# Feed-forward phase: where the second layer's weight pieces are prepared, and how the last layer norm is computed

## The reference, cut to what matters

```
x = _layernorm(x + attn(x));  x = _layernorm(x + xattn(x, ctx));  x = _layernorm(x + ffn(x))

def ffn(x):
    h = (cos(ph) + sin(ph)) * amp          # amp = sigmoid(x @ amp_w + amp_b), ph = pi * tanh(x @ ph_w + ph_b)
    for l in range(2):
        ent = (h @ ent_w[l] + ent_b[l]) @ ent_pw[l] + ent_pb[l]
        h = layer_norm(h + ent, ln3_g[l], ln3_b[l])
        t = sum over two paths of (h @ path_w[l, p] + path_b[l, p]) * (cos(phase[l, p]) + sin(phase[l, p]))
        h = layer_norm(h + t, ln4_g[l], ln4_b[l])
    return h
```

## Time and profile before

| | |
|---|---|
| median of three timed runs | 987.88 us (986.71 to 988.43) |
| profiled execution: its time, its span | 984.96 us, 983.1 us |
| granted TensorE clock over the span | 0.971 of full speed |
| busy: TensorE | 892.4 us, 91% |
| busy: VectorE | 677.2 us, 69% |
| busy: ScalarE | 550.1 us, 56% |
| busy: GpSimd | 496.7 us, 51% |
| first instruction of the feed-forward phase | 652.55 us |

### The profile page before, as it was taken

How to read it: one execution, slowest core, us unless ns; L and a number is a source line. 1 busy time by engine, 2 the same in 40 slices (tenths; PEclk the granted TensorE clock), 3 DMA queues, 4 the chain that set the end, 5 groups by cost and what they waited for, 6 DMA issues and landing times. The chain is left out here.

```text
span 983.1 us, 19518 instructions
## 1 busy us (share of the span) xinstructions
PE 892.4 (91%) x5892; PEld 735.8 (75%) x5892; DVE 677.2 (69%) x2055; ACT 550.1 (56%) x1674; POOL 496.7 (51%) x793
## 2 busy tenths in 40 slices
PE   4999999998898899999999998669899999999893
PEld 4888888887776678778777877457678778778672
DVE  4687778786785777777876766426757657667557
ACT  4756556664664566565755556427564464564461
POOL 0445555455755345454645432610665565566466
PEclk9999999999899999999999999879999999999997
DMA  4644243444665556574654636344002001001001
GB/s 155 222 144 158 98 160 128 160 160 143 210 205 145 168 159 194 166 225 121 188 170 138 181 110 197 132 167 155 0 1 85 3 1 55 32 1 40 4 0 43
DMA packets 79075, 118.53 MB, mean 121 GB/s; under 512 B 7920, under 2 KB 41744, under 8 KB 78224
## 3 DMA queue, kind: packets, MB, share of 16 engines
q1 hardware_dynamic: 78992, 117.52, 37.2%
HBM read 58.76 MB, written 17.83 MB: 78 GB/s over the span
## 5 line engine op out<-in xcount | busy, mean ns | idle before, releaser
L920 ACT ACTIVATE prob<-bank,nmax 128x128 f32<-128x128 f32 (+1 forms) x512 | 209.9, 431 | 38.5 <-DVE nmax L1049 36.9
L161 PE MATMUL bank<-w_ffn,hT 128*128 128x512 f32 x768 | 192.8, 402 | 0.0
L1049 DVE CUSTOM_DVE_ANT_0 bank<-bank,mask 128x128 f32<-128x128 f32 (+1 forms) x512 | 167.6, 383 | 4.0 <-PE bank L1225 3.7
L161 PEld LDWEIGHTS bank<-w_ffn,hT 128*128 128x128 f32 x768 | 141.5, 189 | 30.9
L161 PE MATMUL bank<-xT,w_att 128*128 128x256 f32 x864 | 124.1, 298 | 22.0 <-DVE w_att L961 10.3
L161 PEld LDWEIGHTS bank<-xT,w_att 128*128 128x128 f32 x864 | 115.4, 201 | 31.7 <-DVE xT L1037 9.7
L777 POOL TENSOR_TENSOR zone<-raw,zone 128x256 fp32r<-128x256 f32 x128 | 95.2, 776 | 65.8 <-ACT zone L900 65.8
L1237 PE MATMUL bank<-ident,prob 128*128 128x128 f32 x768 | 119.7, 279 | 4.5 <-ACT probT L933 4.4
L933 ACT ACTIVATE probT<-bank 128x512 f32<-128x512 f32 x97 | 58.3, 603 | 92.7 <-PE bank L1261 91.6
L920 ACT ACTIVATION_READ_ACCUMULATOR prob<-bank,nmax 128x1 f32 x512 | 110.0, 215 | 0.0
L1547 ACT ACTIVATE ht<-bank,cols 128x128 f32<-128x128 f32 x192 | 72.3, 457 | 66.0 <-PE bank L1715 66.0
(11 more groups left out here) (118 smaller groups left out, 1518.7 us busy)
## 6 DMA issues: line engine op xcount, KB each, us to landing
q<-stage SPq DMA_DIRECT2D x192, 128.0 KB, 2.2
k<-kstage SPq DMA_DIRECT2D x48, 256.0 KB, 3.5
x<-xres SPq DMA_DIRECT2D x16, 512.0 KB, 4.0
raw<-in_ent_wT SPq DMA_DIRECT2D x32, 256.0 KB, 3.8
raw<-in_ent_pw SPq DMA_DIRECT2D x32, 256.0 KB, 4.1
raw<-in_xT SPq DMA_DIRECT2D x8, 512.0 KB, 3.6
raw<-in_path_w SPq DMA_DIRECT2D x8, 512.0 KB, 3.7
xres<-in_x SPq DMA_DIRECT2D x8, 512.0 KB, 4.9
```

The costliest lines, as they stand in the source:

```text
L161: ins = t.matmul(out, lhs(a, k), rhs(b, k), start=first and n == 0 and m == 0, stop=last and n == len(kts) - 1 and m == 2, skip_group_chec ...
L920: ins = s.activation(prob[:, u, c * width:(c + 1) * width], banks[u][:, c * width:(c + 1) * width], ACT.Exp, scale=-1.0, bias=nmax[:, i % ...
L1049: ins = v.tensor_tensor_reduce(scored, scored, mask[:, S - width:S], scale=-1.0, scalar=3e38, op0=ALU.add, op1=ALU.min, accum_out=nmax[:, ...
```

## The change

Three things are changed.

- Stages 2 and 3 now also go through the two halves of w_raw. SP loads each of them when VectorE is done with the half's first use, behind the loads of the norm's scale and shift. GpSimd's additions for stage 3 stand behind block 0's second residual.
- Their eight pieces (numbers 8 to 15) are no longer prepared before block 0. ScalarE rounds piece 8+n right behind `hT_of(n)`, and VectorE makes its remainder right behind `unit(n+1)`, for n from 0 to 7, in block 0 alone.
- For the last stage (units 12 to 15) VectorE no longer normalises. Behind the unit's statistics it computes (y - mean)*g in one scalar_tensor_tensor (`centre`), and later y*rstd + (x + b) in a second one (`finish`), then the statistics of the last norm. GpSimd's `last_gain` goes. `finish(i)` moves into `unit(13+i)`, right behind the drain, `NORMS` alternates accordingly, and at a block's end the next block's first two `h0` stand behind the last normalise but one.

```
-    stage_raw = [w_raw[:, 0, :, :], w_raw[:, 1, :, :], y[:, :, :], ht[:, :, :, :].rearrange("p h k j -> p h (k j)")]
+    stage_raw = [w_raw[:, n % 2, :, :] for n in range(2 * NL)]
...
-    NORMS = list(range(UN - 1)) + [UN, UN - 1] + [UN + i for i in range(1, BT)]
+    NORMS = list(range(UN - BT + 1)) + [u for i in range(BT - 1) for u in (UN + i, UN - BT + i + 1)] + [UN + BT - 1]
...
             def load_stage(n):
+                if n >= 2:
+                    wait_alone(q, s_wlo, KT * (n - 1), s_passed)
                 q.dma_start(stage_raw[n], A["fd"][n // 2, n % 2][:, 0:KT, :]).then_inc(s_wraw[n], 16)
...
+            q.dma_start(lng[:, :], A["ln_g"].partition_broadcast(P)).then_inc(s_ln, 16)
+            q.dma_start(lnb[:, :], A["ln_b"].partition_broadcast(P)).then_inc(s_ln, 16)
             load_stage(2)
             load_stage(3)
-            q.dma_start(lng[:, :], A["ln_g"].partition_broadcast(P)).then_inc(s_ln, 16)
-            q.dma_start(lnb[:, :], A["ln_b"].partition_broadcast(P)).then_inc(s_ln, 16)
...
@@ gpsimd, body
-                for u in range(UN - 2):
-                    if 2 <= u:
-                        lo(u - 2)
+                for n, u in enumerate(NORMS):
+                    if 2 <= n < UN - 2:
+                        lo(n - 2)
                     rstd_of(u)
-                    if u < BT:
-                        residual(u)
-
-                last_gain(0)
-                rstd_of(UN - 2)
-                last_gain(1)
...
+                    if n < BT:
+                        residual(n)
+                    if b == 0 and n == 1:
+                        residual_of_path(1)
@@ scalar
+            def piece_hi(k):
+                n, c = divmod(k, KT)
+                if c == 0:
+                    s.wait_ge(s_wraw[n], 16)
+                    if n % 2:
+                        s.wait_ge(s_id, KT * (n // 2 + 1))
+                s.activation(W[:, 0, k * D:(k + 1) * D], stage_raw[n][:, c, :], ACT.Copy).then_inc(s_whi, 1)
...
             gates(k, 0)
-            stage_hi(2)
-            stage_hi(3)
-            s.wait_ge(s_wlo, 2 * NL * KT)
...
                     if kind == "tr":
                         hT_of(n)
+                        if b == 0 and n < 2 * KT:
+                            piece_hi(2 * KT + n)
@@ vector
+            def piece_lo(k):
+                n, c = divmod(k, KT)
+                at = slice(k * D, (k + 1) * D)
+                v.wait_ge(s_whi, k + 1)
+                v.tensor_tensor(W[:, 1, at], stage_raw[n][:, c, :], W[:, 0, at].bitcast(F32), ALU.subtract).then_inc(s_wlo, 1)
...
-            stage_lo(2)
-            stage_lo(3)
             v.wait_ge(s_pbias, 16 * NL)
-            v.wait_ge(s_wlo, 2 * NL * KT)
...
                     k.drain(("mm", u), v.tensor_tensor(y[:, i, :], banks[plan.bank(("mm", u))][:, :], bias[:, s_, :], ALU.add))
-                    if u >= 1:
+                    if u > UN - BT:
+                        finish(u - 1 - (UN - BT))
+                    elif u >= 1:
                         normalise(u - 1, s_norm)
+                    if u > UN - BT + 1:
+                        normalise(UN + u - 2 - (UN - BT), s_fin)
                     k.wait_drained(("mm", u))
                     statistics(u)
+                    if u >= UN - BT:
+                        centre(u)
+
+                def centre(u):
+
+                    i = u % BT
+                    v.wait_ge(s_agg, b * LN + number[u])
+                    v.scalar_tensor_tensor(y[:, i, :], y[:, i, :], mv[:, i, 0:1], lng[:, :], ALU.subtract, ALU.mult).then_inc(s_cen, 1)
 
                 def finish(i):
 
                     n = b * BT + (i + 1)
-                    v.wait_ge(s_g, n)
+                    v.wait_ge(s_rstd, b * LN + number[UN - BT + i])
                     v.wait_ge(s_res, n)
-                    v.tensor_tensor(y[:, i, :], y[:, i, :], xb[b % 2][:, i, :], ALU.add).then_inc(s_sum, 1)
+                    v.wait_ge(s_cen, n)
+                    v.scalar_tensor_tensor(y[:, i, :], y[:, i, :], rstd[:, i, 1:2], xb[b % 2][:, i, :], ALU.mult, ALU.add).then_inc(s_sum, 1)
...
                     if kind == "mm":
-                        if n == UN - 1:
-                            finish(0)
                         unit(n)
+                        if b == 0 and 1 <= n <= 2 * KT:
+                            piece_lo(2 * KT + n - 1)
...
-                finish(1)
-                normalise(UN, s_fin)
-                normalise(UN - 1, s_norm)
-                finish(2)
-                normalise(UN + 1, s_fin)
+                finish(BT - 1)
+                normalise(UN + BT - 2, s_fin)
                 if not last:
                     h0(k, b + 1, 0)
-                finish(3)
-                normalise(UN + 2, s_fin)
-                if not last:
                     h0(k, b + 1, 1)
-                normalise(UN + 3, s_fin)
+                normalise(UN + BT - 1, s_fin)
```

More of the change, by code:

```diff
@@ L1356, in ffn_phase @@
     s_res = sem("s3_res")
-    s_g, s_sum = sem("s3_g"), sem("s3_sum")
+    s_cen, s_sum = sem("s3_cen"), sem("s3_sum")
     s_fin = sem("s3_fin")
@@ L1434, in _, with residual_of_path @@
             g.wait_ge(s_c, 4)
-            for l in range(NL):
+            def residual_of_path(l):
                 g.wait_ge(s_wraw[2 * l + 1], 16)
@@ L1439, in _ @@
                     g.tensor_tensor(own, own, ident[:, :], ALU.add).then_inc(s_id, 1)
+            residual_of_path(0)
             g.wait_ge(s_ln, 32)
@@ L1460, in residual @@
                     g.tensor_tensor(x, x, lnb[:, :], ALU.add).then_inc(s_res, 1)
-                def last_gain(i):
-                    g.wait_ge(s_norm, b * UN + (UN - BT + i + 1))
-                    g.tensor_tensor(y[:, i, :], y[:, i, :], lng[:, :], ALU.mult).then_inc(s_g, 1)
-                for u in range(UN - 2):
-                    if 2 <= u:
-                        lo(u - 2)
-                    rstd_of(u)
-                    if u < BT:
-                        residual(u)
-                last_gain(0)
-                rstd_of(UN - 2)
-                last_gain(1)
[L1476 to L1482, removed]
+                for n, u in enumerate(NORMS):
+                    if 2 <= n < UN - 2:
+                        lo(n - 2)
+                    rstd_of(u)
+                    if n < BT:
+                        residual(n)
+                    if b == 0 and n == 1:
+                        residual_of_path(1)
             every_block(g, body)
@@ L1491, in stage_hi @@
             def stage_hi(n):
-                s.wait_ge(s_wraw[n], 16)
-                if n % 2:
-                    s.wait_ge(s_id, KT * (n // 2 + 1))
                 for c in range(KT):
-                    at = (n * KT + c) * D
-                    s.activation(W[:, 0, at:at + D], stage_raw[n][:, c, :], ACT.Copy).then_inc(s_whi, 1)
+                    piece_hi(n * KT + c)
+            def piece_hi(k):
[5 more added lines that the diff above has]
+                s.activation(W[:, 0, k * D:(k + 1) * D], stage_raw[n][:, c, :], ACT.Copy).then_inc(s_whi, 1)
             def x2T_hi(k, i):
@@ L1582, in stage_lo @@
                 for c in range(KT):
-                    at = (n * KT + c) * D
-                    v.wait_ge(s_whi, n * KT + c + 1)
-                    v.tensor_tensor(W[:, 1, at:at + D], stage_raw[n][:, c, :], W[:, 0, at:at + D].bitcast(F32), ALU.subtract).then_inc(s_wlo, 1)
+                    piece_lo(n * KT + c)
+            def piece_lo(k):
[3 more added lines that the diff above has]
+                v.tensor_tensor(W[:, 1, at], stage_raw[n][:, c, :], W[:, 0, at].bitcast(F32), ALU.subtract).then_inc(s_wlo, 1)
             k = Banks(v, plan_pro, 0)
@@ L1711, in transpose_norm @@
                 def transpose_norm(u):
-                    t.wait_ge(s_norm, b * UN + (u + 1))
+                    t.wait_ge(s_norm, b * (UN - BT) + (u + 1))
                     k.wait_free(("tr", u))
```

## The result

The changed kernel takes 1004.51 us in the median (1003.27 to 1007.4, 6 runs), the kernel before 987.3 us beside it (986.48 to 991.15, 6 runs): 1.0173 times as long, with a 95% interval of 1.0151 to 1.0195. The forecast was 1000.9 us in a range of 996.5 to 1005. So it is slower, by 17.2 us where 13.0 were forecast.

What follows compares the result with a forecast made beforehand. TensorE was taken as the bound, at 3.30 us a unit, until waits between engines set block 0's pace. +14.12 in block 0 and -1.13 in the tail gave +12.99 us: 1000.9 us, own range 998 to 1003.5, full range 996.5 to 1005.

Steps and rivals of the forecast that it cites:

- the circle: Block 0: transposes, ScalarE's scale and piece, VectorE's subtraction, drain, normalise, transposes wait in a ring; 5.31 us a turn against 3.30.
- Rival A: Block 0: the clock falls in every turn, costing 3 us more, time 1004; chance 0.12.
- Rival C: Blocks 0 to 2: slow two-tensor instructions make the next block's gated input late, 1 us each, time 1004; chance 0.07.
- first transposes earlier: Start of block 0: without pieces ahead of unit 0's drain, first transposes come at 691.60 instead of 694.39, 2.79 us won.
- eight turns: Block 0, unit 0's to unit 8's transposes: six plain turns of 5.31 us, two longer of 6.61 and 7.06, 45.53 in all.
- blocks from unit 8 on, without the tail: After the turns: no pieces from unit 9 on, TensorE sets the pace again, blocks 1 to 3 as long as before.
- tail: Last block, after unit 13's drain: the new last norm ends at 979.51 instead of 980.64, 1.13 us won.
- subtraction to the drain behind it 0.61: Step of a block 0 turn on VectorE, priced at 0.61 us because four subtractions in a row take 2.49 us.
- The clock: Block 0: the first long gap should drop TensorE's clock, 0.45 us more on the path, counted once (range 0 to 0.9).
- GpSimd's four additions: Additions to the identity moved behind block 0's second residual: priced at nothing, any delay coming out of the following transposes' gap.
- SP's moved loads: Prologue: loads wait for w_raw's halves, priced at nothing; input issued no later; if cover goes, 1 us or so.
- Rival B: Block 0: pieces fit into VectorE's idle time, so no ring exists; 3.9 us faster, 984.0; chance 0.04.

Runs made afterwards that it cites:

- split_pieces: Against the changed kernel, stage 2's pieces prepared behind the third gate pair, stage 3's subtracted behind units 4 to 7: 983.34 us, 0.9967 times the kernel before.
- split_early_add: As split_pieces, with GpSimd's four additions to the identity for stage 3 moved in front of block 0: 982.24 us, 0.9967 times the kernel before.
- copy_before_scale: Against the changed kernel, ScalarE's rounding of piece 8+n put in front of unit n's scale and shift: 983.42 us, 0.9985 times the kernel before.
- split_early_stats_first: As split_early_add, with units 13 to 15 taking their own statistics ahead of the previous unit's finish: 982.63 us, 0.9977 times the kernel before.
- subtract_later: Against the changed kernel, VectorE's subtraction of piece 8+n put behind unit n+2 instead of n+1: 985.58 us, 0.9994 times the kernel before.
- pieces_before_block: Against the changed kernel, pieces, their loads and GpSimd's additions back in front of block 0, new last norm kept: 987.05 us, 1.0004 times the kernel before.

## Why the prediction was right, and where 4 to 5 us were missing

The direction and the mechanism were right: two runs that open the circle at different places bring the time back, and the chain shows its steps as written. The forecast said 12.99 us from the products' start on, measured are 17.80. The median, 1004.51 us, lies outside the forecast's own range of 998 to 1003.5 and inside 996.5 to 1005 only because that reached over rivals A and C at 1004. Neither of them is the reason for it, so that much was luck. Term by term:

| term | forecast us | measured us |
|---|---|---|
| first transposes earlier | -2.79 | -2.60 |
| eight turns, 45.53 forecast and 48.88 measured, against 28.62 | +16.91 | +20.26 |
| blocks from unit 8 on, without the tail | 0 | +0.50 |
| tail | -1.13 | -0.36 |

**The start.** 5.30 us from products to drain instead of 5.10, then 4.38 for 4.39.

**The turn was mis-sized**, by the step "subtraction to the drain behind it 0.61". It was priced from a row in which GpSimd is idle. On the circle, ScalarE's rounding copy of the unit releases GpSimd's remainder and, half a microsecond later, the piece releases VectorE, so in six of the eight turns GpSimd starts 0.26 to 0.48 us ahead of the subtraction. The subtraction then takes 1.35 to 1.56 us, and the step 1.27 to 1.48 instead of 0.61: 4.2 us in six turns. The other steps were some 0.1 us a turn shorter than added up, which leaves the miss of 3.35 in the turns. The first two turns escaped, 5.28 and 6.45 us against 5.31 and 6.61 forecast. In the first GpSimd was at its four additions, and the subtraction between them took 0.75 us; in the second the subtraction was ahead of GpSimd's remainder. The trace before showed the effect:
```profile
692.79 1.26 POOL L1460 TENSOR_TENSOR xb<-xb,lnb 128x512 f32<-128x512 f32 x1
692.86 1.48 DVE L1620 TENSOR_SCALAR y<-y,mv,rstd 128x512 f32<-128x512 f32 x1 [0.48 <-POOL rstd L1449]
...
701.33 1.30 POOL L1460 TENSOR_TENSOR xb<-xb,lnb 128x512 f32<-128x512 f32 x1
...
701.52 0.69 DVE L1627 TENSOR_TENSOR y<-bank,stage_bias 128x512 f32<-128x512 f32 x1
...
709.45 1.44 POOL L1454 TENSOR_TENSOR hT<-ht,hT 128x512 fp32r<-128x512 f32 x1 [1.00 <-ACT hT L1552]
```
The normalise of 1.48 us stands behind GpSimd; block 1's, as long and in the same place, was taken as work inside the 4.39 us from drain to transposes. The normalise of the earlier trace rows is 0.23 us ahead of GpSimd's remainder (709.45) and keeps 0.54 us, and it is the remainder that takes 1.44. In these rows the engine that starts second pays. The Trainium skill, "VectorE: DVE Perf Modes", section "Two Vector instructions with no wait between them", says that an instruction with two inputs in SBUF, or with one in the faster mode, reads through a second interface that GpSimd shares. The trace agrees: behind GpSimd the subtraction (two such inputs, 0.69 to 1.35) and the normalise (one, 0.54 to 1.19) stretch, and a drain, with one input in PSUM, stays at 0.69 at 701.52. That the normalise runs in the faster mode, no row shows.

**The clock** was counted once, for 0.45 us, and one turn did cost 0.47 more (6.35 against 5.88), but that was luck: the reason given, that the first long gap drops the clock, failed. The transposes behind the longest gap, 3.83 us, ran in 0.66 us, and the ones that took 1.13, at 723.45, came after 2.41. Rival A came true in half: in every second turn the granted clock fell (to between 0.50 and 0.75, read in steps of 3 us), but mostly behind the transposes, where the slower products (4.6 instead of 3.05 us) fill idle time. Of its price of 3 us 0.47 came.

**GpSimd's four additions** were priced at nothing, since "the delay comes out of the gap". In the changed kernel that held, because the gap was there. Once the circle is opened they cost 1.6 us, as split_pieces and split_early_add show. **SP's moved loads** cost nothing, as forecast: the next block's transposes start at 690.00, right behind the products, and the first piece is rounded without a wait for its load. The cover named for GpSimd's additions, though, was a stall that a better version does without.

**The tail** gained 0.36 instead of 1.13 us. The instruction itself was priced well (0.74, measured 0.75). What was left out is GpSimd's rstd: from aggregate to finish it takes 1.72 us at 989.34 to 991.06 and in the unit before, where the sum counted 1.54 with the instructions that stand between, and at the last unit 1.72 for 1.36: 0.72 of the 0.77 us missing. Its first step takes 0.67 us behind VectorE's two-tensor instruction, 0.22 at 718.65 with VectorE idle. Giving it a unit's time won 0.7 us.

**Rival B** (the pieces fit into idle time) named the right condition: with the piece ready when the statistics end, the circle doesn't exist. copy_before_scale fulfils it, and its turns are 29.87 us instead of 48.88. Its price of 3.9 us below the kernel before did not come: 0.9985 times, up to 1.0017, is not to be told from it. **Rival C** did not come: block 1's first drain follows unit 8's transposes after 44.35 us, 44.28 before.

## What to carry to other kernels

Before work is put "behind" a unit, write down what the new instruction waits for and what stands behind it on its engine: if the first goes back to something that the second releases, each pass costs the whole way round, however small the work. Moving it one unit on, or the copy ahead of the wait, opened the circle here and brought back 19 of 20 us. And an instruction's duration is that of its neighbours too: take it from a row in which the other engine is doing what it will be doing there, and look which of the two starts first.

## What the runs showed that I had not expected

The granted clock does not follow the length of one gap. Block 3's first transposes come after the same gap of 2.30 us in nearly all of these profiles; in split_pieces, and in the changed kernel, they and the products behind them ran at full speed, in split_early_add and split_early_stats_first both were at the lower level, 1.2 GHz, for a while (granted 0.53 from 924 to 927 us in the first), and the units behind them lost 1.3 to 1.5 us:
```profile
920.05 0.66 PE L1719 MATMUL bank<-ident,y 128*128 128x128 f32 x4 [2.30 <-DVE y L1617]
923.60 0.66 PE L1719 MATMUL bank<-ident,y 128*128 128x128 f32 x4
```
This is split_pieces; the same place in split_early_add:
```profile
923.95 0.94 PE L1718 MATMUL bank<-ident,y 128*128 128x128 f32 x4 [2.30 <-DVE y L1616]
928.80 0.65 PE L1718 MATMUL bank<-ident,y 128*128 128x128 f32 x4
```
In subtract_later and copy_before_scale the transposes ran in 0.66 us and the products behind them fell (granted 0.50 from 923 to 926 us in the first), for 1.2 us. In the changed kernel a gap of 1.82 us was followed by a stretch at 0.70, and after the longest, of 3.83 us, the transposes still ran in 0.66 us, with the products behind them at 0.50 (713 to 716 us):
```profile
698.00:701.00 3.00, 3.00 (x12) 2.49 (x13) 0.69 (x2) 2.31 (x6) 2.92 (x5) 0.70 0.00 0
```
(a row of the windows view, the stretch behind the gap of 1.82 us; the granted clock is third from last).

One piece of 0.35 us, most of the 0.50 in the table, stays open: between block 2's and block 3's first drains the changed kernel and all versions with pieces among the units take 76.1 to 76.2 us, the kernel before and pieces_before_block 75.8 to 75.9. VectorE pauses for 0.50 us in front of one aggregate there. No run was made on it.
